# Graph attention on one core: the order of products in TensorE's slots, column sums of x on GpSimd, and another PSUM bank for the last pair

## The reference, cut to what matters

```
row_zero  = v.sum(-1) == 0
q_exp     = where(row_zero[..., None], 0.0, q[:, None, :])
self_feat = concat([v, q_exp]) @ W_self.T + b_self
output    = self_feat
for d in range(2):                       # two directions of adj
    A   = adj (d == 0) or adj transposed (d == 1), first 20 columns
    aff = (self_feat @ Wq[d].T + bq[d]) . (self_feat[:, :20] @ Wk[d].T + bk[d]) / sqrt(dh)
    aff = where(A.sum(-1) > 0, aff, -9e15) + (A @ w_bias + b_bias)
    w   = softmax(aff)                   # over the 20 keys, for each head
    output += per head: (w @ self_feat[:, :20]) @ Wout[d].T + bout[d]
out = v + relu(output)
```

## Time and profile before

| | |
|---|---|
| median of 3 runs | 1803.17 us (1800.65 to 1807.22) |
| the profiled execution | 1803.32 us, span 1800.7 us |
| PE busy | 1760.4 us, 98% of the span |
| PEld busy | 1595.1 us, 89% |
| DVE, ACT, POOL busy | 1113.4, 947.5, 777.2 us (62, 53, 43%) |
| mean granted TensorE clock | 0.99 of full |
| chain that ended last | PE 91%, no other engine over 2% |

### The profile page before, as it was taken

One profiled execution on the slowest core, in us unless ns is written; L12 is line 12 of the kernel. 1 busy time (PEld: TensorE's weight loads), 2 busy tenths in 40 slices (PEclk: granted clock), 3 DMA queues, 4 the chain that ended last, 5 costly groups with the idle time before them and its releaser, 6 DMA issues.

```text
span 1800.7 us, 44640 instructions
## 1 busy us (share of the span) xinstructions
PE 1760.4 (98%) x14472; PEld 1595.1 (89%) x14472; DVE 1113.4 (62%) x1812; ACT 947.5 (53%) x1655; POOL 777.2 (43%) x691
## 2 busy tenths in 40 slices
PE   8999999979999999999999999999999999999997
PEld 5899999968988988888888889988888888998885
DVE  2667776866666666666666666666666666666532
ACT  2344444445555555555555555555555555555543
POOL 0444443214444444444444444444444444444444
PEclk9999999979999999999999999999999999999998
DMA  6133334466656554655555556556564655556421
GB/s 212 47 85 85 92 103 111 122 150 168 169 145 171 150 170 135 172 153 155 154 155 157 161 149 188 152 156 169 151 172 143 164 156 155 153 155 182 129 79 57
DMA packets 291516, 258.07 MB, mean 143 GB/s; under 512 B 105968, under 2 KB 221936, under 8 KB 291312
## 3 DMA queue, kind: packets, MB, share of 16 engines
q1 hardware_dynamic: 277920, 244.97, 48.8%
q10 hardware_dynamic: 13392, 10.51, 1.8%
HBM read 199.25 MB, written 56.10 MB: 142 GB/s over the span
## 4 chain that ended last, share of the span: by engine, by line
PE 91%; SPq 2%; issue 2%; DMA 2%; DVE 1%; ACT 1%; POOL 1%; POOLq 0%; ACTq 0%; DVEq 0%
PE bank L1664 29%; PE bank L1678 20%; PE low_banks L939 10%; PE low_banks L1638 9%; PE bank L1699 9%; PE bank L939 5%; PE bank L1691 4%; PE bank L1658 2%; PE bank L486 2%; SPq L1354 1%; PE bank L1706 1%; PE low_banks L462 0%; DMA stage<-in_L_cond_Wq 0%; SPq L658 0%; PE bank L502 0%
## 5 line engine op out<-in xcount | busy, mean ns | idle before, releaser
L1664 PE MATMUL bank<-kx,xt_main 128*128 128x160 f32 x4096 | 599.9, 300 | 0.0
L1664 PEld LDWEIGHTS bank<-kx,xt_main 128*128 128x128 f32 x4096 | 575.8, 191 | 3.0
L1504 POOL TENSOR_TENSOR res<-res,xk 128x512 f32<-128x512 f32 x128 | 163.7, 1279 | 451.5 <-ACT res L1543 451.5
L1561 ACT ACTIVATE wtt<-bank 128x384 f32<-128x384 f32 (+1 forms) x256 | 109.8, 429 | 432.5 <-PE bank L1691 432.5
L1397 DVE TENSOR_TENSOR sc<-bank,masks 128x320 f32<-128x320 f32 x256 | 125.7, 491 | 328.2 <-PE bank L1664 326.2
L1548 ACT ACTIVATE kx<-low_banks 128x1920 f32<-128x1920 f32 (+5 forms) x201 | 306.3, 1524 | 37.4 <-PE low_banks L1638 37.3
L1486 POOL TENSOR_TENSOR sc<-sc,mx 128x640 f32<-128x640 f32 x128 | 160.1, 1272 | 301.5 <-DVE mx L1409 301.5
L1678 PE MATMUL bank<-ws_h,xh_main 128*128 128x512 f32 x512 | 222.1, 434 | 3.5 <-DVE res L1423 3.4
L1638 PE MATMUL low_banks<-key_tile,a_rows 32*128 32x160 f32 (+3 forms) x4288 | 202.8, 315 | 6.4 <-ACT kx L1548 5.8
L1678 PE MATMUL bank<-ws_h,xl_main 128*128 128x512 f32 x512 | 204.7, 400 | 0.0
L1678 PE MATMUL bank<-ws_l,xh_main 128*128 128x512 f32 x512 | 203.2, 397 | 0.0
(11 more groups left out here) (146 smaller groups left out, 2937.6 us busy)
## 6 DMA issues: line engine op xcount, KB each, us to landing
rows_main<-in_x SPq DMA_DIRECT2D x256, 128.0 KB, 3.7
xs<-in_x SPq DMA_DIRECT2D x64, 512.0 KB, 4.7
xk<-in_x SPq DMA_DIRECT2D x64, 512.0 KB, 3.7
res<-c_dram SPq DMA_DIRECT2D x64, 512.0 KB, 5.4
out<-res SPq DMA_DIRECT2D x128, 256.0 KB, 3.4
adj<-in_mask_BxSxSx_ik SPq DMA_DIRECT2D x32, 440.0 KB, 5.3
adj<-in_mask_BxSxSx_ik SPq DMA_DIRECT2D x128, 110.0 KB
vbd<-v_dram SPq DMA_DIRECT2D x768, 10.0 KB
```

Of the source, the lines that this page charges most:

```text
L1504: pool.tensor_tensor(res[:, p.par, b, :], res[:, p.par, b, :], xk[:, p.par, b, :], ALU.add).then_inc(res_ready, 1)
L1664: mm = nc.tensor.matmul(dst, xt[:, j, p.ring + b, :], kx[:, t.par, :, 2 * j:2 * j + 2, w * NG:w * NG + NG] .rearrange("p r c m -> p c r m" ...
```

## The change

There are three edits.

**Order on PE in the long loop.** The flags product is taken out of `scores` into `open_bank`, and stands behind a W_self product for ages 3, 2 and 0. The 12 W_self products of a batch stand in one run. The flag rows are those of pair t, in slot t, behind the values of the late pair, no longer those of the next pair at the end of the slot. The scores of age 0 are made in two parts, one for each batch of the pair, with transposes, mask, generation and values between them. ACT's `flags_out` moves with it, to behind the exponential of batch 1. The new order in a slot is:

flags products ages 3 and 2; scores age 3; transposes (late, 1) part 0; scores age 2; transposes (late, 1) part 1; generate 0; values (late, 1); flag rows of pair t; flags product and scores age 1; generate 1; W_self (soft, 0), all; flags product age 0; transposes (soft, 0) part 0; scores age 0, batch 0; transposes (soft, 0) part 1; mask; generate 2; values (soft, 0); scores age 0, batch 1; W_self (soft, 1).

**Column sums in the keys stage.** POOL adds the four chunks of x in three additions of 320 columns in fp32 (`add_chunks`), each waiting for the one before. PE multiplies the sum with the ones in one fp32 product. The wait for `x_low` moves from the sums to the first feature group.

**The last pair.** In slot 66 batch 0 of pair 63 uses bank 5 in place of `OUT`, and PE has an order of its own (`last_scored`).

```diff
+    def closing(p):
+        return isinstance(p.k, int) and p.n == PAIRS - 1
+
+    def out_bank(p, b):
+        return bank[5 - AGES * PAIRS % 2] if closing(p) and b == 0 else OUT

+        def add_chunks(n, par):
+            pool.wait_ge(x_turned, C * n + C)
+            if due(n):
+                pool.wait_ge(pe_sum, n)
+            for j in range(1, C):
+                if j > 1:
+                    pool.wait_ge(chunks_added, (C - 1) * n + j - 1)
+                pool.tensor_tensor(chunk_sum[:], x_cols(xt, 0, par) if j == 1 else chunk_sum[:], x_cols(xt, j, par),
+                                   ALU.add).then_inc(chunks_added, 1)
...
             by_conditions(n, 7)
             if not tail:
+                add_chunks(n + 2, par)
                 x_lows(n + 2, par)
...
         def sums(n, par):
-            pe.wait_ge(x_low, C * n + C)
-            for j in range(C):
-                for k, part in enumerate((xh, xl)):
-                    mm = nc.tensor.matmul(slot_bank(1 - par, SUM_SLOT), ones[:], x_cols(part, j, par),
-                                          start=(j == 0 and k == 0), stop=(j == C - 1 and k == 1))
-            mm.then_inc(pe_sum, 1)
+            pe.wait_ge(chunks_added, (C - 1) * (n + 1))
+            nc.tensor.matmul(slot_bank(1 - par, SUM_SLOT), ones[:].bitcast(F32), chunk_sum[:],
+                             start=True, stop=True).then_inc(pe_sum, 1)
...
+        def last_scored(t):
+            soft, late = t.back(3), t.back(4)
+            open_bank(t, 3)
+            scores(t, 3)
+            self_features(soft, 0)
+            turn_weights(late, 1, 0)
+            turn_weights(late, 1, 1)
+            values(late, 1)
+            self_features(soft, 1)
+            turn_weights(soft, 0, 0)
+            turn_weights(soft, 0, 1)
+            values(soft, 0)
...
         def slot(t):
             soft, late, nxt = t.back(3), t.back(4), t.back(-1)
+            if soft.n == PAIRS - 1:
+                last_scored(t)
+                return
+            if soft.real():
+                open_bank(t, 3)
+            if t.back(2).real():
+                open_bank(t, 2)
             if soft.real():
                 scores(t, 3)
             if late.real():
-                pe.wait_ge(e_out, t.n + 1 if t.real() else PAIRS)
                 turn_weights(late, 1, 0)
...
             if late.real():
                 values(late, 1)
+            if t.real():
+                if due(t.n):
+                    pe.wait_ge(e_out, t.n)
+                flag_rows(t)
             if t.back(1).real():
+                open_bank(t, 1)
                 scores(t, 1)
             if has_window(nxt):
                 generate(nxt, 1)
             if soft.real():
-                self_features(soft, 0, range(0, 2))
+                self_features(soft, 0)
+            if t.real():
+                open_bank(t, 0)
+            if soft.real():
                 turn_weights(soft, 0, 0)
-                self_features(soft, 0, range(2, C))
+                if t.real():
+                    scores(t, 0, (0,))
                 turn_weights(soft, 0, 1)
...
-                flag_rows(nxt)
             if soft.real():
                 values(soft, 0)
-            if t.real():
+                if t.real():
+                    scores(t, 0, (1,))
+                self_features(soft, 1)
+            elif t.real():
                 scores(t, 0)
-            if soft.real():
-                self_features(soft, 1, range(0, C))
```

More of the change, by code:

```diff
@@ L826, in gpsimd_program @@
             feature_low(0, 0, j)
+        add_chunks(1, 1)
         pool.wait_ge(v["cq_out"], 2 * NK)
@@ L1422, in take_out @@
             dve.wait_ge(pe_out, n + 1)
-            nc.vector.tensor_tensor(res[:, p.par, b, :], OUT[:], res[:, p.par, b, :], ALU.add).then_inc(out_taken, 1)
+            nc.vector.tensor_tensor(res[:, p.par, b, :], out_bank(p, b), res[:, p.par, b, :], ALU.add).then_inc(out_taken, 1)
         def slot(t):
@@ L1641, in generate, with open_bank @@
             mm.then_inc(pe_gen, 1)
-        def scores(t, a):
+        def open_bank(t, a):
             p = t.back(a)
@@ L1657, in scores @@
                 pe.wait_ge(s_added, n - 2)
-            nc.tensor.matmul(s_bank(t, a).rearrange("p (b x) -> p b x", b=2), flags[:, p.c % AGES, :], zu,
-                             start=True, stop=False)
-            for b in range(2):
+            nc.tensor.matmul(s_bank(t, a).rearrange("p (b x) -> p b x", b=2), flags[:, p.c % AGES, :],
+                             zc[:, p.c % AGES, :, o * NQ * NG:(o + 2) * NQ * NG], start=True, stop=False)
+        def scores(t, a, batches=(0, 1)):
+            p = t.back(a)
+            if a == ages(t)[0]:
+                pe.wait_ge(gen_taken, NR * t.n + NR)
+            if a == 0:
+                pe.wait_ge(x_turned, C * (p.n + 1))
+            for b in batches:
                 w = 2 * (AGES - 1 - a) + b
@@ L1666, in scores, with self_features @@
                                           .rearrange("p r c m -> p c r m"), start=False, stop=(b == 1 and j == C - 1))
-            mm.then_inc(pe_s, 1)
-        def self_features(p, b, chunks):
+            if 1 in batches:
+                mm.then_inc(pe_s, 1)
+        def self_features(p, b):
             n = 2 * p.n + b
[L1671 to L1675, removed]
+            if closing(p):
+                if b == 0:
+                    pe.wait_ge(s_added, 4 * PAIRS - 1)
+                else:
+                    pe.wait_ge(out_taken, n - 1)
+            elif due(n):
+                pe.wait_ge(out_taken, n)
+            pe.wait_ge(x_low, n + 1)
+            for j in range(C):
                 h, l = xh[:, j, b, :], xl[:, j, b, :]
                 for k, (a, m) in enumerate(((h, ws_h), (h, ws_l), (l, ws_h))):
-                    mm = nc.tensor.matmul(OUT[:], a, m[:, j, :], start=(j == 0 and k == 0), stop=False)
-            if chunks[-1] == C - 1:
-                mm.then_inc(pe_self, 1)
+                    mm = nc.tensor.matmul(out_bank(p, b), a, m[:, j, :], start=(j == 0 and k == 0), stop=False)
+            mm.then_inc(pe_self, 1)
         def turn_weights(p, b, part):
@@ L1698, in values @@
             for c in range(NW):
-                mm = nc.tensor.matmul(OUT[:, 3 * c * DH:(3 * c + SLOTS) * DH], wtt[:, b, c, :],
+                mm = nc.tensor.matmul(out_bank(p, b)[:, 3 * c * DH:(3 * c + SLOTS) * DH], wtt[:, b, c, :],
                                       vbd[:, p.par, c, :, b * DH:b * DH + DH], start=False, stop=(c == NW - 1))
@@ L1744, in slot @@
                 generate(nxt, 2)
-            if nxt.real():
-                if soft.real():
-                    pe.wait_ge(wtt_ready, 2 * (2 * soft.n + 1))
-                elif due(nxt.n):
-                    pe.wait_ge(e_out, nxt.n)
-                flag_rows(nxt)
             if soft.real():
                 values(soft, 0)
-            if t.real():
+                if t.real():
+                    scores(t, 0, (1,))
+                self_features(soft, 1)
+            elif t.real():
                 scores(t, 0)
-            if soft.real():
-                self_features(soft, 1, range(0, C))
         all_slots(slot, -1)
```

14 lines of the change are left out of this document (7 added, 7 removed).

## The result

The changed kernel takes 1816.22 us (median of 6 runs, 1809.21 to 1819.45), the one before 1801.72 (6 runs, 1799.46 to 1807.22): a ratio of 1.0064, with a 95% interval of 1.0047 to 1.0082 (the quotient of the two medians, 1.0080, lies within it). It is slower by 0.6%. The execution profiled took 1810.86 us (span 1808.7), less than the median; why comes with the experiments.

The account below looks back on a forecast made before the run. PE, dense in keys stage and loop, was taken as the bound; 16.2 + 0.3 - 5.0 - 5.3 = +6.2 us on 1803.3 gave 1809.5 us, 8-in-10 range 1795 to 1819.

Parts of the forecast that it names:

- the part to which it gave 0.37: Whole kernel: slower by over 0.5%, above 1812 us; chance 0.37.
- PE waits for no copy of keys: Sign: the forecast is wrong if PE waits anywhere for a ScalarE copy of keys.
- A change of precision costs nothing: Switches between one-pass and full fp32 products on PE: removing three entries per slot gains 0.00 us, bounds -0.01 to 0.08 each.
- Part 1: Full slots: age-2 flags product ahead of age-3 scores delays the softmax chain to the value products, +0.15 us per slot.
- Part 2: Full slots: flag-row product moved to between values and flags, -0.02 where it was, +0.10 where it goes, +0.08 us together.
- Part 3: Full slots: with half the age-0 scores as cover, W_self(soft, 1) waits for VectorE to empty the OUT bank, +0.04 us.
- The rival with the OUT bank as the bound: Every slot: VectorE empties the bank late and W_self(soft, 1) waits; 0.05 us late is +3, 0.5 is +30; chance 0.18.
- Slots 64 and 65: The two slots after the full ones: only the age-2 flags product's delay counts there, +0.3 us.
- Part 4: Full slots: second transposes wait for the first ones' eviction, covered by three transposes and eight scores (1.42 us): 0.
- Keys stage: Eight column sums of 1.17 us each become one fp32 product of 0.54 each: -5.0 us, bounds -5.6 and 0.
- Last pair: Slot 66's first score to the last value products: 23.95 us becomes 18.7, -5.3 us, bounds -3 and -6.
- PE at half clock again: Last pair: thin work puts PE at half clock, limiting the gain to the bound of -3 us.

Follow-up runs that it names:

- experiments 3 and 4: 3: kernel before, only the age-2 flags product moved ahead of age-3 scores, 1.0055; 4: changed kernel, only that product moved back, 1.0005 to the kernel before.
- experiment 6: Kernel before with only W_self of batch 0 joined in one run and the age-0 scores split: ratio 1.0040 to the kernel before.
- experiment 7: Kernel before with only the keys-stage column sums changed (GpSimd additions, one fp32 product on PE): ratio 0.9977 to the kernel before.

## Why the prediction came out as it did

The forecast was slower by 0.35%, measured was 0.64%, on the side that it named and inside its range. But it held a change under 0.5% for the likeliest (0.53), and what came is just beyond, in the part to which it gave 0.37. The mechanism of the slots held, and from 430 us on PE waits for no copy of keys (at the start of the loop it does, 4.1 us by its products for key generation, 5.8 before). The sizes of two terms outside the full slots did not: slots 64 and 65, and the last pair.

- *A change of precision costs nothing*: right. The flags product of age 2 moved away from the transposes and PE's way past it stayed the same (4.98 and 4.97); W_self joined without a gain; the column sum shows the same early start (0.40 that is really 0.147).
- *Part 1, +0.15*: measured +0.135 and +0.153 in experiments 3 and 4, with a wait of 0.17 on ScalarE's eviction in every slot of the stretch.
- *Part 2, +0.08*: measured +0.09. The term 0.10 is 0.11 by starts (1.45 against 1.34 from values to scores).
 The Trainium skill ("TensorE: Matmul & The Clock Gate", LDWEIGHTS (loading the stationary operand)) prices the load of 128 columns at 107 ns. That the move costs one such load is an estimate from that figure, and the 0.11 of the trace is of its size; no run here parts the load from the product itself.
- *Part 3, +0.04*: measured +0.063 in experiment 6. The gate binds as worked out. By starts, W_self comes 28 ns behind the last score where nothing gates it, 63 in three slots of four of the changed kernel, and 180 in the fourth, where VectorE's eviction begins 0.12 us later: a mean of 0.064 more. The rival with the OUT bank as the bound was this mechanism at a larger size; it decided from 0.05, so a small piece of it came true.
- The three together: +0.305 for +0.27, 2 us over 60 slots.
- *Slots 64 and 65, +0.3*: measured +1.08 and +0.92, 2.0 together. Part 4 put the second transposes' wait at 0 because eight scores of age 0 stand in between. These two slots have no such scores, and there the wait is 0.73.
- *Keys stage, -5.0*: measured -4.45 between first and last projection, and -4.43 in experiment 7. Seven of the eight sums lie between these marks, and 7 x 0.63 is 4.4: the price of one was right.
- *Last pair, -5.3*: this is the term that failed, in three ways. First, it took 23.95 us for the old order, which ran in part at half clock, and 18.7 for the new one, summed at full clock; at full clock the old one is 20.1 by the estimate above, so the order itself is worth 0.7 and not 5.3. Second, the last leg: up to the values of (63, 0) the sum was right (14.99 for 15.3), but from there to the last values it is 4.38 for 3.45. The second transposes of (63, 1) wait 1.66 us and not the 0.73 of other rounds, because the relu of (63, 0) (`clip`, L1567) stands ahead of the first eviction (L1585) in ScalarE's order, and waits itself for VectorE to take the values of (63, 0). In the old order 12 W_self products of (63, 1) covered that. ScalarE in the changed kernel:
```profile
1799.86 0.63 ACT L1567 ACTIVATE res<-res 128x512 f32<-128x512 f32 x1 [2.33 <-DVE res L1447]
1800.39 0.47 ACT L1585 ACTIVATE wtt<-bank 128x384 f32<-128x384 f32 x1
```
 Third, the clock: "PE at half clock again" was a bound of -3, and the mean of the executions is -2.0, the stretch at full clock in three of six.

With the terms as measured: loop +19.9, keys -4.5, last pair -2.0, together +13.4 (+10.8 in the execution with the last pair at full clock), for +6.2 in the forecast. The misses in slots and last pair point the same way, so none cancelled another. The two ratios of the whole change say +11.5 and +11.2, with intervals from 8 to 15, and those of its parts (1.0104 and 0.9962) multiply to 1.0066. The parts of the slot order add up in the slots (0.135 + 0.09 + 0.063 = 0.29 for 0.305). In the ratios they give 0.55 + 0.38 + 0.40 = 1.33% for 1.04%; that surplus of 0.29% is no more than the four intervals allow together (0.30%).

## What to carry to other kernels

Where an engine is dense, ask of each instruction moved whether it now stands ahead of the first link of a chain that ends in a wait of the same engine: there it costs its full length, even though the engine's work is the same; inside the wait of that chain the same instruction is cheap. Price a switch between one-pass and full products by sums from start to start over both, not by the gap at the switch. Where an order leans on a product as cover, look for the slots that lack that product. And where a stretch is short of work for TensorE, read the granted clock of the old stretch before you subtract a new sum from it, and give each clock level a share of the forecast, not the far bound alone.

## What was not expected of the hardware

- A one-pass product behind a full fp32 one is recorded early: behind three transposes the flags product starts after 0.25 us, where 0.33 is due, and the 0.08 come back as 0.23 for 0.15 to the next score; behind the sum of two instructions the projection's start lies 0.25 us ahead of its place.
- One short VectorE operation took nearly five times as long in the changed kernel, and its twin didn't. The line that makes the masks has two forms; this is the one of 80 partitions, by form over the whole execution, the changed kernel first, then before:
```profile
L1284 DVE TENSOR_SCALAR mk<-cn 80x128 f32<-80x128 f32 x32 | 38.0, 1188 | 0.0
```
```profile
L1260 DVE TENSOR_SCALAR mk<-cn 80x128 f32<-80x128 f32 x32 | 7.9, 247 | 0.0
```
 The form 128x80 takes 370 and 369 ns. The long ones come with the joined W_self and split scores (1211 ns in experiment 6), not with the flags product of age 2 or the sums (242, 255). What stretches them wasn't tried. In the loop PE has no wait on them.
- TensorE's clock fell to 1.2 GHz behind waits of 1.01 and 0.85 us in one execution and stayed at 2.4 behind the same two in the other, with the same kernel. The rows of the last pair ahead of it have the same lengths and waits in both (0.73, 1.01, 0.85). What decides it stays open.
